# A deformable-convolution kernel: the deform stage on four strips of whole rows instead of quadrants, its moves as long runs, and the second convolution from chunk 4

## The reference, cut to what matters

```
x = x + conv(gn(x))          # 3x3 depthwise, then three 32x32 matrices: one 3x3 convolution
x = x + deform_conv(gn(x))

def deform_conv(v):
    off = conv3x3(v, w_off)              # 64 outputs: a row and a column offset for every pixel
    rows = clip(r + off_r, 0, H - 1); cols = clip(c + off_c, 0, W - 1)
    # four neighbours (floor and ceil of rows and cols), bilinear mixture of them:
    mapped = fc * (vals_b - vals_t) + vals_t
    return conv3x3(mapped, w_conv) + b_conv
```

## Time and profile before

| | us |
|---|---|
| median of 3 runs (738.85 to 739.9) | 739.05 |
| the profiled execution | 740.63 |
| its span, first to last instruction | 738.8 |
| PE busy | 690.1 |
| DVE busy | 519.5 |
| POOL busy | 491.6 |
| ACT busy | 475.7 |
| mean granted TensorE clock, share of full | 0.981 |

### The profile page before, as it was taken

One profiled execution on the slowest core, in us unless ns is written; L12 is line 12 of the kernel. 1 busy time (PEld: TensorE's weight loads), 2 busy tenths in 40 slices (PEclk: granted clock), 3 DMA queues, 4 the chain that ended last, 5 costly groups with the idle time before them and its releaser, 6 DMA issues. The chain is left out here.

```text
span 738.8 us, 10814 instructions
## 1 busy us (share of the span) xinstructions
PE 690.1 (93%) x3500; PEld 247.4 (33%) x3500; DVE 519.5 (70%) x1031; ACT 475.7 (64%) x841; POOL 491.6 (67%) x434
## 2 busy tenths in 40 slices
PE   4799989999999889998999979999899999997966
PEld 4333333333333233333333333333333333332322
DVE  3687996598954886749955698566985595657592
ACT  7487867785675836676467654667576674876560
POOL 4004968879687486766686575857766849699650
PEclk9999989999999989999999999999999999999998
DMA  8969904999789894989959799696968563657554
GB/s 141 186 102 148 177 10 104 205 145 197 136 195 180 148 200 104 232 146 170 184 133 238 133 166 166 155 220 122 204 127 190 140 148 66 160 109 166 133 123 112
DMA packets 240878, 113.08 MB, mean 153 GB/s; under 512 B 140880, under 2 KB 235184, under 8 KB 239024
## 3 DMA queue, kind: packets, MB, share of 16 engines
q1 hardware_dynamic: 216784, 100.55, 71.0%
q10 hardware_dynamic: 24032, 11.78, 8.4%
HBM read 31.59 MB, written 16.78 MB: 65 GB/s over the span
## 5 line engine op out<-in xcount | busy, mean ns | idle before, releaser
L1317 DVE COPY_PREDICATED other_row<-down_ps,row_diff 128x768 f32<-128x768 int32 x128 | 124.4, 1024 | 139.4 <-ACT down_ps L920 139.1
L715 PE MATMUL off_ps<-x1a,wo 128*64 128x512 f32 x768 | 178.9, 601 | 2.1 <-DVE other_row L1329 2.1
L1115 POOL TENSOR_TENSOR other_row<-other_row,x_quads 128x512 f32<-128x512 f32 x64 | 76.3, 1193 | 154.2 <-DVE other_row L1329 154.2
L715 PE MATMUL off_ps<-x1b,wo 128*64 128x512 f32 x768 | 175.9, 593 | 0.0
L606 PE MATMUL c_ps<-xb,w 128*64 128x512 f32 x336 | 150.8, 598 | 5.6 <-DVE x1a L1301 5.5
L606 PE MATMUL c_ps<-mapb,w 128*64 128x512 f32 x336 | 151.7, 595 | 0.0
L608 PE MATMUL c_ps<-xa,w 128*64 128x512 f32 x336 | 150.8, 598 | 0.0
L909 ACT ACTIVATE other_row<-row_diff 128x768 f32<-128x768 f32 x128 | 101.7, 843 | 68.2 <-POOL row_diff L1101 63.0
L608 PE MATMUL c_ps<-mapa,w 128*64 128x512 f32 x294 | 132.7, 595 | 0.0
L1101 POOL TENSOR_TENSOR row_diff<-x_quads 128x594 f32<-128x594 f32 x64 | 79.5, 1243 | 43.7 <-ACT x_quads L945 43.7
L920 ACT ACTIVATE down_ps<-off_ps,bias_o 128x512 f32<-128x512 f32 x64 | 41.7, 652 | 84.1 <-PE off_ps L715 75.6
(11 more groups left out here) (134 smaller groups left out, 970.4 us busy)
## 6 DMA issues: line engine op xcount, KB each, us to landing
x1b<-x1a SPq DMA_DIRECT2D x28, 520.0 KB, 7.6
mapb<-mapa SPq DMA_DIRECT2D x28, 520.0 KB, 6.9
mapa<-mapped SPq DMA_DIRECT2D x224, 64.0 KB, 2.1
out_dram<-x1a SPq DMA_DIRECT2D x49, 256.0 KB, 4.7
x_quads<-x1a SPq DMA_DIRECT2D x192, 65.0 KB, 3.1
xb<-in_x_dram SPq DMA_DIRECT2D x48, 256.0 KB, 8.1
xa<-in_x_dram ACTq DMA_DIRECT2D x40, 256.0 KB, 6.8
xa<-in_x_dram SPq DMA_DIRECT2D x16, 256.0 KB, 6.9
```

What stands on the lines that cost most here:

```text
L715: last = nc.tensor.matmul(off_ps[k % 2][64 * t:64 * t + 64, CH * n:CH * n + CH], wo[wpar][:, kx, 64 * t:64 * t + 64], rows[:, 4 * k:4 * k ...
L1115: step(pool.tensor_tensor(split(column), split(column), own, ALU.add))
L1317: last = dve.copy_predicated(other_row[n][:, :, KR // 2 * odd:KR // 2 * odd + KR // 2, :], bass.AP(tensor=rows.tensor, offset=rows.offset ...
```

## The change

- **Strips.** Each 32 partitions take a strip of 32 whole rows instead of a quadrant. `x1_quads` becomes `x1_strips`, with four planes (row mod 4) of whole rows of 130 floats: one tile for the upper half of all strips, and two, used in turn, for the lower half. `mapped` gets whole rows with pad columns too.
- **Moves.** `move_strip` and `move_rows` move runs of 4 or 5 whole rows (520 or 650 floats a partition). There are still 16 DMAs for each half. For image 0 the moves leave the pads out.
- **Place of the moves.** Both halves of the strips of image i+1 are now moved in the second half of image i; before, the second half of `x1_quads` was moved at the start of image i+1, ahead of `move_mapa(1)`.
- **Pads.** The pads of `x1a` are filled before its rows are moved (`pad_x1`, one call), and SP waits for that (`x1_pads`) ahead of `copy_x1b`. `pad_mapped` fills the pads of `mapped`.
- **Row differences.** One call of `row_steps` does two chunks in two instructions of 792 and 330 elements, in place of 594 for each chunk.
- **Order.** The second convolution starts at chunk 4 with two groups each; its first group waits for both halves. In image 7 five groups of image 6 run in chunks 2 to 6, and three are left over for the time after chunk 7.
- **Groups of images 6 and 7** are spread: group g takes the blocks g, g+8, g+16, g+24.
- **End.** The first half goes by DMA as before. Of the second half, SP moves the left columns (after chunk 5) and copies all of these rows to `xb`; after that (`end_copied[1]`) ACT, POOL and DVE copy the right columns in 32 instructions. Five groups wait for all of it.

```
-    SECOND_CONV1 = [[3], [4, 5], [6, 7], [], [], [], [], []]
-    LAST_CONV2 = [[], [], [], [0], [1], [2, 3], [4, 5], [6, 7]]
-    END_CONV2 = [[], [], [0], [1], [], [2, 3], [4, 5], [6]]
-    CONV2_GROUPS = [1, 5, 0, 4, 2, 6, 3, 7]
-    STORE_AFTER = [7, 8]
-    END_GROUPS = [1, 5, 2, 6, 3, 0, 4, 7]
-    END_PARTS = [0, 0, 1, 1, 2, 2, 2, 2]
+    SECOND_CONV1 = [[3], [4, 5], [6], [7], [], [], [], []]
+    LAST_CONV2 = [[], [], [], [], [0, 1], [2, 3], [4, 5], [6, 7]]
+    END_CONV2 = [[], [], [0], [1], [2], [3], [4], []]
+    CONV2_GROUPS = [0, 2, 4, 6, 1, 3, 5, 7]
+    STORE_AFTER = [6, 8]
+    BEFORE_END_GROUPS = [1, 2, 3, 0, 4, 5, 6, 7]
+    END_GROUPS = [1, 2, 3, 4, 5, 6, 7, 0]
+    END_PARTS = [0, 0, 0, 1, 1, 1, 1, 1]
+    COPY_END_BEFORE = 3
...
-        x1_quads = sb("x1_quads", [P, HQ + 2, WQP])
+        x1_strips = [sb(f"x1_strips{n}", [P, STRIP]) for n in range(3)]
-        mapped = sb("mapped", [P, HQ, WQ])
+        mapped = sb("mapped", [P, 4, NJ, WP])
...
+        def strips_of(i, half):
+            return x1_strips[0 if half == 0 else 1 + i % 2]
...
+        STRIP_PLANES = ((0, 0, 5), (1, 0, 4), (2, 0, 4), (3, -1, 5))
+        def move_strip(queue, i, half, strip):
+            par, to = i % 3, strips_of(i, half)
+            p_to = Q * (2 * (strip % 2) + strip // 2)
+            for q, first, n in STRIP_PLANES:
...
+                    queue.dma_start(to[p_to:p_to + Q, at:at + n * WP],
+                                    x1a[par][p:p + Q, b:b + n, :].rearrange("p b w -> p (b w)"))
...
                     sp.wait_ge(mapped_ready, NK * i)
-                    move_quads(sp, i % 3, 1)
                     if i >= 2:
                         sp.wait_ge(conv2_done, 8 * (i - 1))
+                    sp.wait_ge(mapped_pads, 2 * i)
                     move_mapa(1)
...
-                    sp.wait_ge(x1_ready, 8 * (i + 1) + 5)
+                    sp.wait_ge(x1_pads, i + 2)
                     sp.wait_ge(off_done, NK * i + 4)
                     copy_x1b((i + 1) % 3, 0)
-                    sp.wait_ge(x1_ready, 8 * (i + 1) + 8)
-                    sp.wait_ge(mapped_ready, NK * i + 5)
-                    move_quads(sp, (i + 1) % 3, 0)
+                    sp.wait_ge(mapped_ready, NK * i + 4)
+                    for half in range(2):
+                        move_strips(sp, i + 1, half)
...
-                    move_end()
-                    sp.wait_ge(end_moved, 16 * DMA)
-                    copy_end()
+                    move_rows(xa, 0, 4, end_moved[0])
+                    sp.wait_ge(end_moved[0], A_MOVES * DMA)
+                    copy_rows(xb, xa, 0, 4, end_copied[0])
+                    sp.wait_ge(mapped_pads, 2 * i + 2)
+                    sp.wait_ge(mapped_ready, NK * i + 6)
+                    move_left_columns(end_moved[1])
+                    sp.wait_ge(end_moved[1], A_MOVES * DMA)
+                    copy_rows(xb, xa, 4, 4, end_copied[1])
+                    sp.wait_ge(out_ready, 8 * i)
...
             def conv2(i, wpar, m, ps):
-                if m in (0, 2):
+                halves = [m // 3] if spread(i) and m in (0, 3) else range(2) if not spread(i) and m == 0 else []
+                for half in halves:
...
-                                                    wo[wpar][:, kx, 64 * t:64 * t + 64],
-                                                    rows[:, 4 * k:4 * k + 4, kx:kx + W],
+                                                    wo[wpar][:, kx, side:side + 2 * C],
+                                                    rows[:, b:b + 7:2, kx:kx + W],
...
-                act.wait_ge(diff_ready, g + 1)
+                act.wait_ge(diff_ready, 2 * (g // 2 + 1))
...
+                    if k == 1:
+                        pad_mapped(i, i % 3, 0)
+                        if prev:
+                            clamp(i, 1)
+                    if k == 5:
+                        pad_mapped(i, i % 3, 1)
...
+                    if nxt and k and 7 in conv1_groups(i, k - 1):
+                        pad_x1(i + 1, (i + 1) % 3)
...
-            def row_steps(i, k):
+            def row_steps(i, pair):
+                u = NK // 2 * i + pair
...
+                pool.tensor_tensor(diff[:, 0:12 * WQP].rearrange("p (q j w) -> p q j w", q=3, j=4),
+                                   rows(PLANE, inner), rows(0, inner), ALU.subtract).then_inc(diff_ready, 1)
...
-                    if k + 2 < NK:
-                        row_steps(i, k + 2)
+                    if k % 2 == 0 and k < NK - 2:
+                        row_steps(i, k // 2 + 1)
...
+            def copy_end_rows():
+                dve.wait_ge(end_copied[1], B_MOVES * DMA)
+                dve.wait_ge(mapped_ready, NK * NB)
+                for which in END_SHARES["dve"]:
```

More of the change, by code:

```diff
@@ L353, in store_group, with move_strips, strips_count @@
+        def move_strips(queue, i, half):
+            for strip in range(4):
+                move_strip(queue, i, half, strip)
+        def strips_count(half, i):
+            return DMA * STRIP_MOVES * (i + 1)
         def store_group(queue, i, par, g, rows=(1, 2, 3, 0)):
             image = out[i].rearrange("c (b r) w -> c b r w", r=4)
-            b, e = 4 * g, 4 * g + 4
             for q in rows:
-                first = 1 if q == 0 and g == 0 else 0
-                n, r = (b - 1, 3) if q == 0 else (b, q - 1)
-                queue.dma_start(image[:, n + first:n + 4, r, :], x1a[par][Q * q:Q * q + Q, b + first:e, 1:W + 1])\
-                     .then_inc(end_stored, DMA)
@@ new lines, in copy_x1b, with move_rows @@
+                sp.dma_start(to_upper[:, :, of], upper[:, :, of]).then_inc(x1b_copied[half], DMA)
+            def move_rows(tile, first, n, moved):
+                for q in range(4):
+                    for strip in range(4):
+                        p, b = Q * (2 * (strip % 2) + strip // 2), NJ * strip + first
+                        sp.dma_start(tile[Q * q:Q * q + Q, b:b + n, :].rearrange("p b w -> p (b w)"),
+                                     mapped[p:p + Q, q, first:first + n, :].rearrange("p b w -> p (b w)"))                          .then_inc(moved, DMA)
@@ new lines, in move_left_columns @@
+            def move_left_columns(moved):
+                for q in range(4):
+                    for t in range(2):
+                        for o in range(2):
+                            p = Q * (2 * t + o)
+                            b = NJ * (2 * o + t) + 4
+                            sp.dma_start(xa[Q * q:Q * q + Q, b:b + 4, 0:1 + WQ],
+                                         mapped[p:p + Q, q, 4:8, 0:1 + WQ]).then_inc(moved, DMA)
+            def copy_mapb(half):
+                copy_rows(mapb, mapa, 4 * half, 4, mapb_copied[half])
@@ L750, in _ @@
                     offsets_bias(v, 0, 0, c_ps[2])
-                    pe.wait_ge(x1_pads, 2 * v + 2)
+                    pe.wait_ge(x1_pads, v + 1)
+                    for half in range(2):
+                        pe.wait_ge(x1b_copied[half], COPIES * DMA * v)
                     for k in range(NK):
@@ L1005, in _ @@
                 if nxt and FURTHER_BIAS[i] < NK - 1 or i + 2 == NB:
[L1006 to L1007 removed]
                     clamp(i + 1, 0)
[L1009 to L1015 removed]
+            act.wait_ge(end_copied[1], B_MOVES * DMA)
+            act.wait_ge(mapped_ready, NK * NB)
+            for which in END_SHARES["act"]:
+                to, rows = end_row(*which)
+                last = act.activation(to, rows, ACT.Copy)
+            last.then_inc(end_rows["act"], 1)
             for m in (0, 2, 4, 6):
@@ L1032, in _ @@
                         x1_group(v, 0, 0, m, False, c_ps[m % 2])
-                    pad_x1(v, 0, 0)
-                    pad_x1(v, 0, 1)
+                    pad_x1(v, 0)
+                    for half in range(2):
+                        pad_mapped(v, 0, half)
                     offset_biases(v, 0, c_ps[2])
```

404 lines of the change are left out of this document (194 added, 210 removed).

## The result

The changed kernel takes 743.13 us (median of 5 runs, 742.95 to 743.99), the kernel before 739.36 beside it. The ratio is 1.0052, with a 95% interval of 1.0037 to 1.0066: slower by half a per cent, where 732.2 was forecast. In a later set it was 744.46 against 739.76, 1.0067 (1.0049 to 1.0086). The profiled execution has a span of 742.0 us, the one of the later set 743.0.

What follows compares the result with a forecast made beforehand. PE, the busiest engine, was taken to be as fast as SP's full queue of moves lets it be. The span of 738.8 us, -17.5, +11 and -0.3, gave 732.0, so 732.2 for the median; range 727 to 737, chance 0.50.

Steps and rivals of the forecast that it cites:

- the term for image 1: PE's first group in image 1: a new wait for mapb of 9 us, bounds 5.5 and 12, plus 2 of clock, +11.
- the end: Image 7 and the end, counted from its first offsets: 105.6 us in place of 105.9, 0.3 less.
- Images 2 to 5: PE's waits for mapb there and the clock lost behind them: all 17.0 us removed, with a margin of 2.7.
- 82.7 - 6.5 = 76.2: SP's chain in images 2 to 5, pads to mapb's landing: 82.7 us before, less 6.5 of 8 gained.
- So I put every new move at the old 0.61: SP's issue of moves: longer runs issue no faster, 0.61 us each, 0.66 with the gap.
- By the rows, no: Moves within SBUF: longer runs don't make them cheaper; 231 and 228 GB/s for a full share in two windows.
- the 4.0 us which I gave to the loads of xb being out of the way: SP's 16 issues of x1 moves: 10.52 us in a free queue, 14.53 directly behind the loads of xb.
- Why small descriptors are slow (HBM only): Skill section cited on the moves' transfer: transfers within SBUF don't suffer the penalty of short runs.
- 17.4 with the clock's loss, less 2.6: PE's last groups: six took 17.4 us before, so the five that remain take 14.8.
- Image 1 doesn't wait: Rival: whole rows issue in 0.42 us, not 0.61, so mapb is in time in image 1; 721.2 us, chance 0.20.
- SP's chain stays the bound: Rival: gains of 6.5 us in images 2 to 5 don't come; 750.8 us, or 741 with half; chance 0.20.
- the deform engines bound thin chunks: Rival: in images 0, 1 and 7 later differences cost 1 us for two chunks; 738 us, chance 0.10.

Runs made afterwards that it cites:

- short_runs: Changed kernel with every move of strips (except image 0's) and of mapa cut into runs of 65 floats: 768.83 us, 1.0413 of the kernel before.
- late_xa: Changed kernel with ACT's last four loads of xa in image 1 issued behind chunk 4, not chunk 3: 740.2 us once, 753.4 to 755.9 three times.
- half1_behind_mapb1: Changed kernel with the 16 moves of image 1's lower strips issued behind image 0's second copy to mapb, clamped behind chunk 3: 754.88 us, 1.0223 of before.
- half1_behind_mapa0: Changed kernel with the 16 moves of image 1's lower strips issued behind image 0's mapa(0) moves, clamped behind chunk 3: 743.66 us, 1.0076 of before.
- both kernels of chunk 5: Changed kernel with the second convolution starting behind chunk 5, not 4: for image 0 alone 750.60 us, in images 1 to 6 748.25 us.
- split_mapa1: half1_behind_mapa0 with 8 of the 16 last moves of image 0's mapa issued by ACT in chunk 1 of image 1: 738.43 us, 0.9984 of before.
- chunk5_small_xa: conv2_chunk5 with ACT's loads of xa in images 1 to 5 cut to one block of 16, as many DMAs: 735.08 us, 0.9938 of before.
- conv2_chunk5: Changed kernel with the second convolution behind chunks 5 to 7 (3, 3 and 2 groups) in images 1 to 6: 748.25 us, 1.0109 of before.
- chunk5_late_xa: conv2_chunk5 with ACT's second four loads of xa issued behind chunk 4, not chunk 3, in images 1 to 5: 750.51 us, 1.0131 of before.

## Why the prediction was wrong

**The step that failed** is the term for image 1: +11 (a wait of 9 us, bounds 5.5 and 12, and 2 of clock) measured 14.4 + 2.4 = 16.8. The mechanism was right, the size was not: the landing of mapa's last moves was put at 2 to 4 us and took 6.4, and the 32 moves of strips ahead of it were put at 21.1 us and took 23.9. The rest of the miss is the end (-0.3 was put, +3.2 and in the second profile +1.6 measured), 0.6 of pace, and 0.9 because the median lies 1.1 above the profiled span and not 0.25.

*Images 2 to 5* went as forecast: 17.5 us gone, the first groups 83.45 apart (83 to 84 was said), and SP's rest ahead of `x1b`. The pads came 78.95 us ahead of the need (434.09 to 513.04), as worked out (426.3 to 505.2). From 350.65 to the second mapb's issue it was 66.6, with 7.5 for landing 74.1, where 82.7 - 6.5 = 76.2 was put: a margin of 4.9 in place of 2.7. But one reason was wrong. "So I put every new move at the old 0.61" holds for the issue, "By the rows, no" doesn't hold for the transfer. The two windows of the earlier trace rows gave 231 and 228 GB/s for a full share, at different mixes of other traffic; over the whole kernel it is 210 with long runs against 188, and without them waits in images 2 to 6 come back: from image 1 to 6 it is 436.1 us in place of 418.9. As for the 4.0 us which I gave to the loads of xb being out of the way: SP issues the 32 moves of an image in 23.2 to 24.1 us with long runs and in 24.7 to 27.7 with short ones, so part of it, perhaps all, was the runs. That the term came out at -17.5 is therefore luck in part: it needed the long runs, to which the prediction gave nothing. The rule of the Trainium skill, DMA: Bandwidth & Descriptors, Why small descriptors are slow (HBM only), was weighed as agreeing that transfers within SBUF don't suffer; short_runs speaks against it in this kernel.

*Image 1.* SP's path was worked out as far as the last move's issue, at 163.6 against a bound of 163; the 32 moves of strips took 23.9 us where 32 x 0.66 = 21.1 was put. Then comes the landing of the last moves of mapa. It was put at 2 to 4 us, although the prediction itself names a landing of 5.8 us beside ACT's loads of xa, and ACT issues four of them here too, from 160.5 on. It took 6.4. Without these loads it is 1.4 us, in late_xa and in half1_behind_mapb1. With 7.5 us for mapb, as assumed, this gives 177.5, 3 us above the upper bound of 174.5. PE reached the wait at 164.82 and not at 162.4 because of its wait for `w2`, which I did not see; half1_behind_mapa0 shows that it costs nothing while mapb is later. Against the need at 162.4, mapb is 15.2 us late, and the clock costs 1.7 more.

*The end* was said to cost 0.3 less. The length of PE's wait was right (9 us were forecast, 9.12 met), its end was 84.8 us after image 7's start in place of 83.3: chunk 5 was mapped 0.7 later, and the 16 moves of left columns took 11.5 us in place of 10.5. The landing, the copies to xb and ACT's part each came within 0.4 us of what was put.

The clock behind the pause is the other half of the 3.2. In the first profile of the changed kernel the first seven pairs of matmuls took the lower level:

```profile
722.84 1.03 PE L651 MATMUL c_ps<-xb,w 128*64 128x512 f32 x1
...
723.69 0.61 PE L651 MATMUL c_ps<-xb,w 128*64 128x512 f32 x1
```

That is 6.0 us at 1.06 in place of 0.59 us an instruction (the pairs begin 0.86 us apart in place of 0.43), after a pause of 9.12; before, after one of 5.48, PE was at the higher level from 717.33 on, 3.2 us behind the pause. But the length of the pause does not explain this. In the second profile of the same kernel, after one of 8.88, PE is back at the higher level after 3.1 us:

```profile
720.06 1.09 PE L651 MATMUL c_ps<-xb,w 128*64 128x512 f32 x1 [8.88 <-ACT xb L1065]
...
723.19 0.59 PE L651 MATMUL c_ps<-xb,w 128*64 128x512 f32 x1
```

There the five groups take 15.0 us to DVE's last, where 14.8 was said, against 16.6 in the first profile, and the rest is 107.5 in place of 109.1. So the "17.4 with the clock's loss, less 2.6" that I had carried over holds in one execution and not in the other. What both show is the later end of the pause and a tail of 7.7 and 7.9 us in place of 7.5.

*The rivals.* "Image 1 doesn't wait", with 721, needed an issue of 0.42 us for a strip's move; it took 0.591. Whether PE would have kept such a lead was not tried. In half1_behind_mapb1, the profile of late_xa and both kernels of chunk 5 PE came ahead by edits that left SP its work, SP's round grew to between 84.6 and 87.5 us (90.3 once), and images 2 to 5 gave the lead back, by waits for mapb or for stores. In split_mapa1, where SP has 8 issues less, PE kept its 6.4 us. "SP's chain stays the bound" had the right reason, "the stalls are owed to bytes in the queue" (chunk5_small_xa takes 1.9 MB an image away and the lead holds), but in the changed kernel as it is SP keeps pace in images 2 to 5, with a rest in each. That the deform engines bound thin chunks is not seen; ACT's and POOL's waits in image 1 are for SP's moves.

In short, the change did not remove the limit, it moved it: in their first profiles both kernels reach image 7 at 632.9, the one with five short waits, the other with a long one. What is not settled: why a round that starts late is longer by more than its loads (in conv2_chunk5 the strips, mapa and mapb took 70.7 us from `x1b` to mapb in image 3, in the changed kernel 66.5), and why late_xa's runs fall into two groups. Nor was any of this tried with the short moves of before.

## What to carry to other kernels

Where an engine waits in each round for a queue that is full, find the round's length of that queue, not the sizes of the waits: edits that move issues change where the engine waits, and only edits that took issues or bytes from the queue made image 7 start earlier. Before forecasting a gain of one engine, ask what the other does in the rounds that follow when it has lost its pause. Look also at what a moved load collides with, and at who needs its data. And before a difference of 2 or 3 us is given to the clock, read a second profile of the same kernel.

## What the runs showed of the hardware

- With moves within SBUF in runs of 65 floats (260 B) in place of 520 to 650, the DMA engines were used 12% longer (553 against 496 us of all engines for 104.18 MB, of which the moves are 32.7), while the issue differed by 0.026 us.
- SP's eight loads of 256 KB took 10.1 to 11.5 us to issue where ACT's four loads came at least 5 us later, and 15.0 to 16.6 us where they came within a microsecond (255.90 and 255.71 in half1_behind_mapb1). With ACT's loads cut to a sixteenth it was 11.4 us at 2 us of distance (chunk5_small_xa). A queue's stall can thus be caused by another queue's bytes.
- The lower level of TensorE's clock behind the pause at the end (until the first matmul of about 0.6 us) lasted 3.1 to 6.0 us after pauses of 8.6 to 9.4 us (11 profiles) and 3.1 to 5.8 after pauses of 4.8 to 5.5 us (6 profiles): 6.0 and 3.1 in the two profiles of one kernel.
- Near a balance of two rounds (83.45 and 84 to 88 us) small shifts decide: late_xa's four runs lie at 740.2 and 753.4 to 755.9, chunk5_late_xa's from 743.8 to 754.8, while the changed kernel's stay within 743.3 to 745.4 in one set.
